# Attention on one core: the output projection and the accumulation of a block in slot 1, four blocks behind, instead of in slot 6, three behind

## The reference

```python
c_q  = h_t @ W_DQ + b_DQ
c_kv = h_t @ W_DKV + b_DKV
q = concat(c_q @ W_UQ + b_UQ, c_q @ W_QR + b_QR)      # 8 heads
k = concat(c_kv @ W_UK + b_UK, h_t @ W_KR + b_KR)
v = c_kv @ W_UV + b_UV
attn = softmax(q k^T / sqrt(160))
x = x + (attn v over the heads) @ W_O + b_O
```

## Time and profile before

| | us |
|---|---|
| median of 3 runs | 732.03 (731.91 to 733.4) |
| the profiled execution | 736.64 |
| its span | 734.8 |
| PE busy in it | 712.6 (97%) |
| DVE busy | 582.3 (79%) |
| ACT busy | 459.9 (63%) |
| POOL busy | 540.0 (73%) |

### The profile page before, as it was taken

The page is one execution under the profiler, slowest core; times in us unless marked ns, Lnnn a source line. Parts: engine busy times, 40 slices in busy tenths (PEclk is TensorE's granted clock), DMA queues, the critical chain, the costliest instruction groups (busy, mean ns, idle before and its releaser), DMA issues.

```text
span 734.8 us, 12898 instructions
## 1 busy us (share of the span) xinstructions
PE 712.6 (97%) x4488; PEld 478.5 (65%) x4488; DVE 582.3 (79%) x1213; ACT 459.9 (63%) x1069; POOL 540.0 (73%) x440
## 2 busy tenths in 40 slices
PE   7999999999999999999999999999899999999997
PEld 6665566566566566566566556576666699778885
DVE  8878888888888888888888887844988636878885
ACT  4367777677677677677677666643777831455553
POOL 6468988989988988988988988513689861446774
PEclk9999999999999999999999999997999999999999
DMA  6323676466466466466466474040000000022430
GB/s 150 89 51 66 115 138 122 87 137 123 87 137 123 88 136 124 86 137 124 86 137 123 88 143 88 1 118 2 1 2 1 1 2 1 1 87 74 145 100 30
DMA packets 38853, 61.55 MB, mean 84 GB/s; under 512 B 14456, under 2 KB 23689, under 8 KB 34948
## 3 DMA queue, kind: packets, MB, share of 16 engines
q0 software_dynamic: 11936, 46.14, 32.2%
q1 hardware_dynamic: 25572, 14.47, 7.3%
q10 hardware_dynamic: 1280, 0.12, 0.1%
HBM read 13.35 MB, written 1.10 MB: 20 GB/s over the span
## 4 chain that ended last, share of the span: by engine, by line
PE 60%; DVE 20%; POOL 10%; issue 8%; ACT 1%; DMA 0%; POOLq 0%; DVEq 0%
DVE mx L1091 16%; PE ps L1560 16%; PE ps L1516 10%; PE ps L1502 8%; POOL hid_lo L1037 5%; PE ps L1544 5%; PE ps L1921 4%; POOL nrm L1017 2%; PE ps L1580 2%; PE ps L1961 2%; PE ps L1963 2%; PE ps L1962 2%; POOL hid L1017 1%; PE ps L1489 1%; PE ps L1490 1%
## 5 line engine op out<-in xcount | busy, mean ns | idle before, releaser
L1091 DVE TENSOR_REDUCE mx<-ps 128x1 f32<-128x512 f32 x492 | 302.9, 683 | 59.4 <-PE ps L1502 59.4
L649 ACT ACTIVATE prob<-ps 128x512 f32<-128x512 f32 x512 | 261.6, 628 | 17.9 <-PE ps L1516 13.9
L1516 PE MATMUL ps<-q_cols,key 128*128 128x512 f32 x512 | 210.0, 413 | 0.6 <-ACT prob L649 0.4
L1502 PE MATMUL ps<-key,q_rows 128*128 128x512 f32 x512 | 202.9, 400 | 0.8 <-DVE key L1077 0.4
L1516 PEld LDWEIGHTS ps<-q_cols,key 128*128 128x128 f32 x512 | 95.4, 187 | 70.9 <-issue 33.2
L1560 PE MATMUL ps<-prob,val 128*32 128x512 f32 x1024 | 123.3, 598 | 0.0
L935 POOL TENSOR_TENSOR part<-prob 128x512 f32<-128x512 f32 x84 | 115.2, 1509 | 6.9 <-ACT prob L649 6.7
L949 POOL TENSOR_TENSOR pair<-prob 128x512 f32<-128x512 f32 x60 | 86.8, 1464 | 41.9 <-ACT prob L649 41.9
L1502 PEld LDWEIGHTS ps<-key,q_rows 128*128 128x128 f32 x512 | 95.6, 188 | 18.8 <-DVE mx L1085 1.4
L1037 POOL TENSOR_TENSOR hid_lo<-hid,hid_hi 128x512 fp32r<-128x512 f32 x44 | 61.5, 1409 | 38.7 <-ACT hid_hi L815 38.6
L1560 PEld LDWEIGHTS ps<-prob,val 128*32 128x32 f32 x1024 | 26.7, 109 | 54.2 <-issue 49.5
(11 more groups left out here) (292 smaller groups left out, 1234.5 us busy)
## 6 DMA issues: line engine op xcount, KB each, us to landing
part<-prob POOLq DMA_DIRECT2D x20, 1024.0 KB, 7.2
w_v<-prob POOLq DMA_DIRECT2D x10, 1024.0 KB, 7.4
part<-part POOLq DMA_DIRECT2D x19, 512.0 KB, 5.3
w_v<-w_v POOLq DMA_DIRECT2D x9, 512.0 KB, 5.6
g_all<-g_rows SPq DMA_DIRECT2D x9, 256.0 KB, 3.2
g_all<-g_rows SPq DMA_DIRECT2D x6, 224.0 KB, 3.0
X<-in_L_attn_h_t_dram SPq DMA_DIRECT2D x4, 256.0 KB, 4.3
out_dram<-X SPq DMA_DIRECT2D x4, 256.0 KB, 2.7
```

The lines of the kernel that those rows point to most:

```text
L649: act.activation(prob[:, g % RING, :], ps[:, g % 3, :], ACT.Exp, scale=SCALE).then_inc(s_exp, 1)
L1091: dve.tensor_reduce(mx[:, n % 2, c % TPB, at:at + 1], ps[:, BANK["rows", 2 * lin + j], :], AX.X, ALU.max).then_inc(s_mrd, 1)
L1502: pe.matmul(ps[:, BANK["rows", 2 * lin + j], :], q_rows[:, k, i * P:(i + 1) * P], key[:, h % KBUF, c0:c0 + BLK], start=True, stop=True).th ...
L1516: pe.matmul(ps[:, g % 3, :], key[:, n // NB % KBUF, t * P:(t + 1) * P], q_cols[:, n % NB, :], start=True, stop=True).then_inc(s_sc, 1)
```

## The change

The list of banks, DVE's order and PE's order are changed in the same way. For blocks 4 to 29 slot 1 has `output(n - 4)` on PE, behind the two row tiles and ahead of the second half of the weighted sum, and `denominators(n - 4)` and `accumulate(n - 4)` on DVE, behind the maxima of the slot and `keys_lo`. Slot 6 of blocks 3 to 28 has neither; in block 29 `output(n - 3)` stays there, and from block 30 on all is as it was. What an output's item displaces in the list changes who has which bank.

```diff
@@ the list of banks
-                if (slot == 6 and 3 <= n < NBLK - 2) or (slot == 3 and n == NBLK - 2):
+                if slot == 1 and 4 <= n < NBLK - 2:
+                    todo.append(("out", n - 4))
+                if (slot == 6 and n == NBLK - 3) or (slot == 3 and n == NBLK - 2):
                     todo.append(("out", n - 3))
@@ DVE
-                        if (slot == 6 and 3 <= n < NBLK - 2) or (slot == 3 and n == NBLK - 2):
+                        if slot == 1 and 4 <= n < NBLK - 2:
+                            denominators(n - 4)
+                            accumulate(n - 4)
+                        if (slot == 6 and n == NBLK - 3) or (slot == 3 and n == NBLK - 2):
                             denominators(n - 3)
                             accumulate(n - 3)
@@ PE
-                        if (slot == 6 and 3 <= n < NBLK - 2) or (slot == 3 and n == NBLK - 2):
+                        if slot == 1 and 4 <= n < NBLK - 2:
+                            output(n - 4)
+                        if (slot == 6 and n == NBLK - 3) or (slot == 3 and n == NBLK - 2):
                             output(n - 3)
```

## The result

The changed kernel takes 724.58 us (median of 4 runs, 724.42 to 726.85), the kernel before, on the same chip and with one run more than ahead of the prediction, 731.97. The ratio is 0.989, with a 95% interval from 0.987 to 0.992: faster by 1.1%. The profiled execution took 724.64 us, its span is 722.8.

What follows compares the result with a forecast made beforehand. PE was taken to bound the attention part, with a hole ahead of slot 6's output. 1.27 us removed less 0.94 added gives 0.33 us a block, 8.6 us over 26 blocks: 732.03 to 723.4 us, range 721.0 to 728.0.

Steps and rivals of the forecast that it cites:

- What bounds the kernel: PE bounds the attention part; its one hole is slot 6's output waiting for DVE's seventh maximum, 11.1 us over 27 blocks.
- What leaves slot 6: Without the output, last row tile to weighted sum on PE shrinks from 1.64 to 0.37 us: 1.27 us removed a block.
- What comes into slot 1: The output ahead of slot 1's weighted sum adds 0.94 us a block: 0.88 without a wait, 0.06 waiting for DVE.
- The sum of 0.33 us a block: Net gain of a block, 1.27 - 0.94 us; over 26 blocks 8.6 us.
- DVE's accumulation for nothing: The accumulation moved into slot 1 costs nothing, ending about 347.1 with 0.5 us left before slot 2's maxima.
- POOL: Its adds of slots 2 and 3 move back 0.94 us; 1.27 of 1.44 us waiting is used, 0.17 left, no cost.
- The shift as what is late next: The maxima's DMA, needed by the next block's first score, keeps a margin of 0.25 us, 1.27 less than before.
- The first rival, margins partly spent: Shift's DMA or POOL's margin breaks, costing some 0.15 us on average: 4.7 us gained, 727 us; chance 14%.
- An output costs 0.88 us where it doesn't wait: In slot 1, 1.21 us for an output without a wait less today's 0.33 us makes 0.88 us added.
- The lock between DVE and POOL: Rival: the accumulation in slot 1 is held by POOL's adds, a block grows about 0.7 us, 742 us; chance 4%.

Runs made afterwards that it cites:

- the first experiment: The kernel before, with slot 6's output on PE behind the first half of the weighted sum instead of ahead: 730.54 us against 731.36, ratio 0.998.

## Why the prediction was right, and by how much not

It said 723.4 us, within 721.0 to 728.0; measured were 724.58. Step by step:

- **What bounds the kernel.** Right. The wait for DVE's seventh maximum was the hole, and its size of 0.43 us was measured by itself.
- **What leaves slot 6: 1.27 us.** Right: 1.64 - 0.37.
- **What comes into slot 1: 0.94 us, with 0.06 us of it a wait.** Right: 1.28 - 0.33 = 0.95 us. The release came 337.95 - 337.76 = 0.19 us behind the row product's start; worked out were 0.18.
- **The sum of 0.33 us a block.** A little too much. The block lost 0.295 us. Of the 0.035 us, 0.005 to 0.01 is in slot 1. On the mean of the blocks with keys the way in slot 6 is 1.63 us before and 0.38 after, so 1.25 us left it and not 1.27. The rest, 0.01 us, is spread over the small products of slots 2 to 6 and isn't placed. The 24 blocks with keys made 7.1 us where 7.9 were counted.
- **DVE's accumulation for nothing.** Right: 0.60 us were left (0.5 worked out). One reduction more cost nothing and three cost their excess. The rate at which lateness reaches PE, all but 0.1 us of it, held too.
- **POOL.** Right to 0.1 us: 1.30 and 0.17 us of waiting.
- **The shift as what is late next.** Right that it is next, and right in size: 0.25 us were worked out, and the load has 0.26 us to spare, with 0.08 us more at least that the product takes without loss. Five waits stand in place of two. A landing of 2.8 us was priced at 0.65 us for its block; one of 2.7 us cost 0.4. What the prediction didn't have is the other margin of the same DMA: behind POOL's large one it lands 5 us late or more. This was no part of the change, whose 0.74 us between the two issues stayed.
- **The first rival, margins partly spent.** It didn't come about: POOL's 0.17 us and the shift's 0.26 us held in all blocks but one.
- **An output costs 0.88 us where it doesn't wait.** For slot 1 this is borne out, since the change gives the output the same neighbours as those in the earlier trace rows, a row product ahead and 32-column products behind. Taking it for any place was the mistake of the first experiment's theory: the runs show 0.90 us among products of 128 columns and 1.22 us among products of 32.
- **The lock between DVE and POOL.** It didn't happen: the accumulation, 339.94 to 341.07, lies wholly inside POOL's adds of 338.42 to 341.41, and took 1.13 us, as before. The trace agrees with what the Trainium skill says of a DVE instruction with one SBUF input outside the two-port modes, that it doesn't contend with GpSimd (SBUF — State Buffer, section "Who interferes with whom").

## What to carry to other kernels

When banks go round in the order of a hand-written list, each item waits for the reader of the one that many places back: look there for a short, regular wait of the busiest engine, and move the item to where that reader has caught up. Price it between the same neighbours, and check how small the margins behind it become: here 7.4 us were gained, and making one small DMA wait for two more maxima cost 193 us in one kernel and 215 in the other. A small DMA that somebody waits for has to have its packets out ahead of those of a large one on another queue, and how far ahead is a margin to write down. A margin is best read as the time from a landing to the weight load that needs it, which the trace has.

## What the runs showed of the hardware

- A DMA of 2 KB issued by SP 0.31 to 0.36 us behind an adding DMA of 1 MB issued by POOL took 7.0 us to landing (median of that run's 32, up to 8.4), against 1.9 us when it was issued 0.73 us ahead of it. The packets of the two alternate, 16 of each queue in every 0.6 us: eight small packets on each DMA engine wait for eight large ones of 0.63 us.
- A product of 128 columns behind products of 32 columns started 1.85 us after sixteen of those, where one of 32 columns started after 1.74, and the output there took 1.09 us to what follows instead of 0.98: the first weight load starts with its product, as if it had waited for a semaphore.
- A weight load held by a wait costs more than the idle time ahead of its product: the output of the earlier trace rows started 0.32 us late, and what follows it came 0.43 us late.
- A weight load that came 0.08 us late behind a DMA cost nothing, since its product usually starts 0.23 us behind it.
- Four operations of DVE with a PSUM and an SBUF tensor took 1.13 us wholly beside two adds of POOL, and the adds 2.99 us, as in the run with the output behind the weighted sum, where no such operation ran beside them (329.81, 2.99 us).
